# Linear attention beside a gather: the gates go from GpSimd to ScalarE, and GpSimd's adds move one iteration on

## The chip, the cores and the metric

The kernel runs on one core of a Trainium2 chip. The metric is the device time of one execution in microseconds. Before the change the median of three runs is 2528.86 us (2523.08 to 2537.23). The profiled execution took 2537.77 us, its span from the first to the last instruction is 2536.0 us, so 1.8 us lie around the span. All durations below come from that execution.

## The reference

Two transformer layers on X of shape 8 x 1024 x 128 (8192 tokens). What the change touches is the seam between them: the end of the first layer's mixture of experts, and the second layer's attention.

```
# layer 0, experts: every token has two experts with the gates w0, w1
out0 = all_out[n, top2_i[:, 0]]
out1 = all_out[n, top2_i[:, 1]]
moe_out = w[:, 0:1] * out0 + w[:, 1:2] * out1
result = clip(x + moe_out, -100, 100)        # x: the normalised token
# layer 1, linear attention, 16 heads of 8, causal sums over the tokens
q, k = relu(x Wq) + EPS, relu(x Wk) + EPS ;  v = x Wv
kv_cum = cumsum(k outer v) ;  k_cum = cumsum(k)
out = (q . kv_cum) / (q . k_cum + EPS) ; y = out @ Wo.T
```

Then a router picks one of eight experts for each token.

## The kernel before, in words

The program is a row of stages, each a block with one instruction stream per engine, kept in step by semaphores: projections, softmax attention, routing, experts of layer 0, `linear` (the stage of the change), capacity, experts of layer 1. The order of the instructions is written out by hand; no scheduler moves any.

`linear` works on 64 tiles of 128 tokens, four tiles to a group, so 16 groups. `groups` runs `iteration(g)` on every engine: four iterations (-2 to 1) written out, a loop of six rounds with two iterations each (groups 2 to 13), four more written out. In iteration g, for t = 0 to 3, the engines do the following.

- GpSimd: `keep_state(g, t)` (two small products, once ScalarE has copied the running sum, `raw`), then `outer` for the next tile (t+1, or tile 0 of the next group): the outer products k x v of a tile, 1024 columns. At t = 0 it copies the slot numbers of group g+2 (`take_slots`), and at t = 0, 1, 2 it issues 3, 3 and 2 indirect DMAs (`gather`) that fetch two expert rows for each of the 512 tokens of group g+2. At t = 3, `gate(g+2)`: multiply the rows by their gates (L1400), add the two rows of a token (L1404), add the normalised token (L1408), giving `moe`.
- VectorE: `features` of the next tile (L1685), `attend_tile(g, t)` (L1692 to L1718), and at t = 0 the block that begins with `clip(g+1)` (L1647), which waits for `moe` of group g+1, with `add_moe`, the statistics of the first norm and seven steps of the router between them. At t = 1 and 2 come the scales of both norms.
- ScalarE: `keep_sums` (`raw`, L1582), `keep_values` of the next tile (`v`, L1588 and L1589), `keep_queries` (`qT`, L1595), and at certain t roots, exponentials, whole-group copies and the normalised rows (`normalise`, L1610).
- TensorE: per tile the running state, the projection two tiles ahead, the turned q, the causal sums `p_cum` (`sums`, L1481) from the outer products and the share of the earlier tiles, `p_prev` (L1493).

The handovers that matter below: `outer` waits for `v`, `v` for `features`; `sums` waits for `outer`; `attend_tile` waits for `sums`; `keep_state` waits for `raw` and for `p_prev`; `clip` waits for `moe`. The rows and slots have two buffers, `moe` has one; the gate values lie in `GATE` for all tokens.

Of the kernel before, what the change touches and what calls it, by code (L numbers as in the profile page):

```python
# [22 lines left out]
ALU = mybir.AluOpType  # L23
# [3 lines left out]
P = 128  # L27
# [3 lines left out]
G = 4  # L31
# [36 lines left out]
def apart(eng, sem, value, passed):  # L68

    eng.wait_ge(sem, value)  # L70
    eng.sem_inc(passed, 1)  # L71
# [1197 lines left out]
def linear(nc, c, X, XN, GATE, SLOT, BESTP, HOT, W1, w, ys):  # L1269
# [5 lines left out]
    with ExitStack() as ctx:  # L1275
        def sb(name, shape, dt=F32):
            return ctx.enter_context(nc.sbuf_tensor(f"ln_{name}", shape, dt))
# [3 lines left out]
        def ps(name, shape):  # L1281
            return ctx.enter_context(nc.psum_tensor(f"ln_{name}", shape, F32))

        wqkv, wo, wr = sb("wqkv", [P, 3 * D]), sb("wo", [P, D]), sb("wr", [P, E1])
        slot = [sb(f"slot{i}", [P, G * 2], I32) for i in range(2)]
        rows = [sb(f"rows{i}", [P, G * 2, D]) for i in range(2)]
        moe = sb("moe", [P, G, D])

# [18 lines left out]
            "w_in", "ones", "mask", "x_a", "x_c", "stats_a", "stats_c", "var_a", "var_c", "root_a", "root_c",  # L1307
            "rstd_a", "rstd_c", "xn_a", "xn_c", "pxT_a", "pxT_c", "xT_a", "xT_c", "qkv", "qk", "v", "pqT", "qT",
            "kc", "kv", "st", "raw", "state", "cum", "prev", "prod", "o", "poT", "oT", "y", "kept", "logits", "shift",
            "exp", "passed", "w1_in", "moe", "clip", "den", "num", "slots", "gated", "top", "router")}  # L1310
        rows_in = [sem(f"rows_in{i}") for i in range(2)]
        passed = S["passed"]
        block = ctx.enter_context(nc.Block())
# [5 lines left out]
        def number(g):  # L1319
            return g[0] * 2 + g[1]  # L1320
# [43 lines left out]
        @block.gpsimd  # L1364
        def _(pool):
            def masked(out, keys, reps):

                nc.gpsimd.memset(out, 1.0).then_inc(S["mask"], 1)
                pool.wait_ge(S["mask"], keys + 1)
                nc.gpsimd.affine_select(out=out, in_=out, compare_op=ALU.is_ge, fill=0.0, base=0,  # L1370
                                        pattern=[[-DH1, H1], [0, reps]], channel_multiplier=1).then_inc(S["mask"], 1)
                pool.wait_ge(S["mask"], keys + 2)
                nc.gpsimd.affine_select(out=out, in_=out, compare_op=ALU.is_ge, fill=0.0, base=DH1 - 1,
                                        pattern=[[DH1, H1], [0, reps]], channel_multiplier=-1).then_inc(S["mask"], 1)

            masked(own_head[:, 0:D].rearrange("p (h m) -> p h m", h=H1), 0, DH1)
            masked(own_head[:, D:D + H1].rearrange("p (h m) -> p h m", h=H1), 3, 1)
            for i in range(2):
                nc.gpsimd.memset(v1[i][:, D:D + 1], 1.0).then_inc(S["ones"], 1)

            def take_slots(g):

                n, i = number(g), g[1]
                nc.gpsimd.tensor_copy(slot[i][:, :], SLOT[:, bass.ds(n * G * 2, G * 2)]).then_inc(S["slots"], 1)
                apart(pool, S["slots"], n + 1, passed)
                if not (isinstance(n, int) and n < 2):
                    apart(pool, S["moe"], n - 1, passed)

            def gather(g, t):
                i = g[1]  # L1390
                for n in ((0, 1, 2), (3, 4, 5), (6, 7), ())[t]:
                    pool.indirect_dma_start(rows[i][:, n, :], None, ys[:, :],  # L1392
                                            bass.IndirectOffsetOnAxis(ap=slot[i][:, n:n + 1], axis=0)).then_inc(rows_in[i], 16)

            def gate(g):
                b, i = g
                n = number(g)
                two = rows[i][:, :, :].rearrange("p (t k) d -> p t k d", k=2)
                apart(pool, rows_in[i], (b + 1) * G * 2 * 16, passed)
                nc.gpsimd.tensor_tensor(rows[i][:, :, :], rows[i][:, :, :],  # L1400
                                        GATE[:, bass.ds(number(g) * G * 2, G * 2)].unsqueeze(2).broadcast_to([P, G * 2, D]),
                                        ALU.mult).then_inc(S["gated"], 1)
                pool.wait_ge(S["gated"], 2 * n + 1)
                nc.gpsimd.tensor_tensor(two[:, :, 0, :], two[:, :, 0, :], two[:, :, 1, :], ALU.add).then_inc(S["gated"], 1)  # L1404
                if not (isinstance(n, int) and n == 0):
                    apart(pool, S["x_a"], n, passed)
                apart(pool, S["gated"], 2 * n + 2, passed)
                nc.gpsimd.tensor_tensor(moe[:, :, :], two[:, :, 0, :], group_of(XN, g), ALU.add).then_inc(S["moe"], 1)  # L1408

            def keep_state(g, t):  # L1410
                n = tile_number(g, t)
                apart(pool, S["raw"], n + 1, passed)
                if not (isinstance(n, int) and n == 0):
                    apart(pool, S["prev"], prevs(g[0], g[1] * G + t), passed)
                nc.gpsimd.tensor_tensor(state[:, 0:D], raw[:, 0:D], own_head[:, 0:D], ALU.mult).then_inc(S["state"], 1)
                nc.gpsimd.tensor_tensor(state[:, D:D + H1], own_head[:, D:D + H1], raw[:, D:D + 1].broadcast_to([P, H1]), ALU.mult).then_inc(S["state"], 1)

            def outer(g, t):
                n = tile_number(g, t)
                pool.wait_ge(S["v"], n + 1)  # L1420
                from_first(pool, "cum", n - 1)
                shape = [P, H1, DH1, DH1]
                k = qk[t % 2][:, D:2 * D].rearrange("p (h d) -> p h d", h=H1)
                v = v1[t % 2][:, 0:D].rearrange("p (h m) -> p h m", h=H1)
                nc.gpsimd.tensor_tensor(kv[t % 2][:, 0:KV1].rearrange("p (h m d) -> p h m d", h=H1, m=DH1),  # L1425
                                        k.unsqueeze(2).broadcast_to(shape), v.unsqueeze(3).broadcast_to(shape),
                                        ALU.mult).then_inc(S["kv"], 1)

            def iteration(g):
                for t in range(G):  # L1430
                    nxt = next_tile(g, t)
                    if exists(g):
                        keep_state(g, t)
                    if exists(nxt[0]):
                        outer(*nxt)
                    if exists(after(g, 2)):
                        if t == 0:
                            take_slots(after(g, 2))
                        gather(after(g, 2), t)
                        if t == 3:  # L1440
                            gate(after(g, 2))

            pool.wait_ge(S["mask"], 6)
            pool.sem_inc(passed, 1)
            groups(pool, iteration)
# [112 lines left out]
        def _(act):  # L1558
# [42 lines left out]
            def normalise(g, k):  # L1601
# [9 lines left out]
                                                bias=shift[k][:, t:t + 1], scale=rstd[k][:, t:t + 1])  # L1611
                last.then_inc(S[f"xn_{k}"], 1)

            def iteration(g):
                before = after(g, -1)
                for t in range(G):
# [20 lines left out]
                        normalise(after(g), "a")  # L1637
                    if t == 2 and exists(before):
                        normalise(before, "c")

            groups(act, iteration)

# [425 lines left out]
```

## Time and profile before

| | |
|---|---|
| median of 3 runs | 2528.86 us |
| the profiled execution | 2537.77 us |
| its span | 2536.0 us |
| TensorE busy | 1976.8 us (78%) |
| VectorE busy | 1680.6 us (66%) |
| ScalarE busy | 1055.1 us (42%) |
| GpSimd busy | 1688.4 us (67%) |
| granted TensorE clock, mean | 0.867 of full speed |

The shares are means over stages with different limits. The linear stage runs from about 1687 to about 2175 us of the span. A timeline row gives the start of an instruction in microseconds from the span's start, its duration, engine, line, operation and tiles, and in brackets how long the engine had been idle before it and what released it ("issue" where the profile shows nothing that it waited for). A start that follows another by less than that one's duration means that the two overlap in the pipeline.

### The profile page before, as it was taken

How to read it: one execution, taken by the hardware profiler on the slowest of the kernel's cores; microseconds unless marked ns; L12 is line 12 of the kernel's file. 1: busy time of each engine (PE TensorE's matmuls, PEld its weight loads, DVE VectorE, ACT ScalarE, POOL GpSimd, SP SyncE). 2: the span in 40 equal slices, each digit the busy share in tenths (PEclk: the TensorE clock that was granted, in tenths of full speed). 3: DMA queues.
4: the chain of work that ended last, by engine and by line, in shares of the span. 5: the costliest groups of instructions: out<-in, count | busy, mean ns of one | idle time of the engine just before them, and what ended most of it. 6: DMA issues, size and time to landing. Idle time of an engine off the chain costs nothing. (4 is left out here: it accounts for less than half of the span.)

```text
span 2536.0 us, 48665 instructions
## 1 busy us (share of the span) xinstructions
PE 1976.8 (78%) x12588; PEld 1077.1 (42%) x12588; DVE 1680.6 (66%) x4398; ACT 1055.1 (42%) x1662; POOL 1688.4 (67%) x1184
## 2 busy tenths in 40 slices
PE   7969999999999999999764529956667777320698
PEld 3423333333333333333254518843344444210597
DVE  7857777777777777777365653426888888550354
ACT  4534555555555555555432315522444444112243
POOL 3436888888888888888736553348887875117365
PEclk9878999999999999999865559978998889555799
DMA  6763222222222122222022223440000000112232
GB/s 196 252 211 107 66 65 60 59 65 66 66 65 64 59 62 66 66 66 64 22 85 74 98 73 118 128 153 24 18 20 20 19 17 9 38 54 98 77 103 69
DMA packets 159727, 192.97 MB, mean 76 GB/s; under 512 B 28793, under 2 KB 113792, under 8 KB 159648
## 3 DMA queue, kind: packets, MB, share of 16 engines
q1 hardware_dynamic: 144816, 161.83, 20.8%
q0 software_dynamic: 13824, 29.43, 3.6%
q10 hardware_dynamic: 1008, 0.92, 0.1%
q14 instruction: 60, 0.49, 0.1%
q8 instruction: 19, 0.31, 0.1%
HBM read 110.48 MB, written 82.10 MB: 76 GB/s over the span
## 5 line engine op out<-in xcount | busy, mean ns | idle before, releaser
L598 DVE TENSOR_REDUCE halfmax<-p_m 128x1 f32<-128x512 f32 x1024 | 664.2, 680 | 246.8 <-PE p_m L486 245.6
L467 POOL TENSOR_TENSOR sum_p<-sum_p,probs 128x1024 f32<-128x1024 f32 x320 | 754.7, 2358 | 39.9 <-ACT probs L593 19.7
L593 ACT ACTIVATE probs<-p_s 128x1024 f32<-128x1024 f32 x512 | 522.2, 1024 | 484.1 <-PE p_s L511 400.8
L486 PE MATMUL p_m<-ka,qa 128*128 128x512 bf16 x1024 | 397.0, 388 | 39.3 <-DVE halfmax L598 18.4
L510 PE MATMUL p_s<-qa,ka 128*128 128x512 bf16 x1024 | 391.4, 382 | 1.5 <-ACT probs L593 0.9
L511 PE MATMUL p_s<-qb,kb 66*128 66x512 bf16 x1024 | 390.9, 382 | 0.0
L518 PE MATMUL p_o<-probs,vh 128*32 128x256 f32 x4096 | 274.0, 385 | 0.0
L467 POOL TENSOR_TENSOR sum_p<-probs 128x1024 f32<-128x1024 f32 x64 | 150.3, 2348 | 138.1 <-ACT probs L593 138.1
L1481 PE MATMUL ln_p_cum<-ln_kv,c_tri 128*128 128x512 f32 (+1 forms) x384 | 167.4, 579 | 55.6 <-POOL ln_kv L1425 55.6
L1051 POOL DMA_INDIRECT xs<-r_xn,r_slot x128 | 124.6, 973 | 120.5 <-DVE r_slot L1015 85.4
L486 PEld LDWEIGHTS p_m<-ka,qa 128*128 128x128 bf16 x1024 | 99.6, 97 | 244.4 <-DVE halfmax L598 150.0
L1135 ACT ACTIVATE e_h<-e_p_h,e_w 128x256 f32<-128x256 f32 x316 | 126.4, 474 | 164.2 <-PE e_p_h L1114 90.3
L510 PEld LDWEIGHTS p_s<-qa,ka 128*128 128x128 bf16 x1024 | 100.1, 98 | 177.6 <-issue 99.8
L1114 PE MATMUL e_p_h<-e_xT,e_w 128*128 128x256 f32 x632 | 162.6, 392 | 5.0 <-DVE e_xT L1129 5.0
L1122 PE MATMUL e_p_y<-e_w,e_h 128*128 128x128 f32 x1264 | 163.2, 277 | 3.0 <-ACT e_h L1135 3.0
L518 PEld LDWEIGHTS p_o<-probs,vh 128*32 128x32 f32 x4096 | 106.8, 109 | 127.8 <-issue 44.4
L1392 POOL DMA_INDIRECT ln_rows<-ys,ln_slot x128 | 125.4, 979 | 46.4 <-issue 27.5
L1122 PEld LDWEIGHTS e_p_y<-e_w,e_h 128*128 128x128 f32 x1264 | 151.5, 193 | 7.6 <-issue 7.2
L1107 PE MATMUL e_p_xT<-c_ident,e_xb 128*128 128x128 f32 x236 | 46.7, 281 | 134.1 <-DMA e_xb<-xs 134.1
L1175 POOL DMA_INDIRECT out<-e_y,e_row_of x80 | 92.0, 1150 | 79.5 <-DVE e_y L1149 63.3
L1481 PEld LDWEIGHTS ln_p_cum<-ln_kv,c_tri 128*128 128x128 f32 x384 | 78.6, 219 | 155.9 <-issue 130.7
L511 PEld LDWEIGHTS p_s<-qb,kb 66*128 66x128 bf16 x1024 | 99.4, 97 | 93.4 <-issue 1.9
(277 smaller groups left out, 3110.3 us busy)
## 6 DMA issues: line engine op xcount, KB each, us to landing
qa<-q SPq DMA_DIRECT2D x128, 128.0 KB, 2.6
ka<-k SPq DMA_DIRECT2D x128, 128.0 KB, 2.8
e_xb<-xs SPq DMA_DIRECT2D x40, 257.0 KB
e_xb<-xs SPq DMA_DIRECT2D x78, 128.0 KB, 2.0
ys<-e_y SPq DMA_DIRECT2D x78, 128.0 KB, 1.9
v<-pj_v SPq DMA_DIRECT2D x8, 1024.0 KB, 5.0
qb<-q SPq DMA_DIRECT2D x64, 128.0 KB, 2.8
kb<-k SPq DMA_DIRECT2D x64, 128.0 KB, 2.9
```

What stands on the lines that cost most here:

```text
L467: nc.gpsimd.tensor_tensor(sum_p[s % 2][:, :], (sum_p[s % 2] if n else probs[0])[:, :], probs[k][:, :], ALU.add).then_inc(sum_p_d, 1)
L486: nc.tensor.matmul(max_bank(s, n)[:, :], qa[s][:, (n // 2) * P:(n // 2 + 1) * P], ka[s][:, (n % 2) * HALF:(n % 2 + 1) * HALF], start=True, ...
L510: nc.tensor.matmul(p_s[k % 2][:, q], ka[s][:, cols], qa[s][:, q], start=True, stop=False)
L511: mm = nc.tensor.matmul(p_s[k % 2][:, q], kb[s][:, cols], qb[s][:, q], start=False, stop=True)
L518: mm = nc.tensor.matmul(p_o[s % 2][j * DH0:(j + 1) * DH0, col, :], lhs, rhs[:, j * Q:(j + 1) * Q], start=start, stop=stop, skip_group_chec ...
L593: nc.scalar.activation(probs[k][:, :], p_s[k % 2][:, :], ACT.Exp, scale=SCALE).then_inc(probs_d, 1)
L598: nc.vector.reduce_max(halfmax[s % 2][:, n % 2, n // 2:n // 2 + 1], max_bank(s, n)[:, :], AX.X).then_inc(max_read, 1)
L1114: mm = nc.tensor.matmul(p_h[s % 2][:, f, :], w1[s][:, f * P:(f + 1) * P], xT[s % 2][:, :], start=True, stop=True)
L1122: mm = nc.tensor.matmul(p_y[s % 2][:, t * P:(t + 1) * P], h[s % 2][:, f, t * P:(t + 1) * P], w2[s][:, f, :], start=(f == 0), stop=(f == NF ...
L1135: last = nc.scalar.activation(h[s % 2][:, f, :], p_h[s % 2][:, f, :], act_fn, bias=b1[s][:, f:f + 1])
L1392: pool.indirect_dma_start(rows[i][:, n, :], None, ys[:, :], bass.IndirectOffsetOnAxis(ap=slot[i][:, n:n + 1], axis=0)).then_inc(rows_in[i] ...
L1481: mm = nc.tensor.matmul(p_cum[:, a, 0:z], c["tri"][:, :], kv[t % 2][:, a * 512:a * 512 + z], start=True, stop=True)
```

## The change

ScalarE gets a new function `weigh(g)`: eight activations (Identity) that multiply the eight row blocks of a group, 128 x 128 each, by the gate as a scale per partition. It is called at the end of t = 3, for group g+2 in iteration g, and waits for the gathered rows. GpSimd loses the multiply (L1400), keeps the two adds (now `gate(g+1)`) and does them at t = 0 of the next iteration, behind `keep_state` and `outer` of that t and ahead of `take_slots`. [...] `gated` now counts groups weighed by ScalarE, and `pair` is a new semaphore for GpSimd's first add.

```diff
--- before.py
+++ after.py
@@ -1283,6 +1283,7 @@
 
         wqkv, wo, wr = sb("wqkv", [P, 3 * D]), sb("wo", [P, D]), sb("wr", [P, E1])
         slot = [sb(f"slot{i}", [P, G * 2], I32) for i in range(2)]
+        share = [sb(f"share{i}", [P, G * 2]) for i in range(2)]
         rows = [sb(f"rows{i}", [P, G * 2, D]) for i in range(2)]
         moe = sb("moe", [P, G, D])
 
@@ -1307,7 +1308,7 @@
             "w_in", "ones", "mask", "x_a", "x_c", "stats_a", "stats_c", "var_a", "var_c", "root_a", "root_c",
             "rstd_a", "rstd_c", "xn_a", "xn_c", "pxT_a", "pxT_c", "xT_a", "xT_c", "qkv", "qk", "v", "pqT", "qT",
             "kc", "kv", "st", "raw", "state", "cum", "prev", "prod", "o", "poT", "oT", "y", "kept", "logits", "shift",
-            "exp", "passed", "w1_in", "moe", "clip", "den", "num", "slots", "gated", "top", "router")}
+            "exp", "passed", "w1_in", "moe", "clip", "den", "num", "slots", "gated", "pair", "top", "router")}
         rows_in = [sem(f"rows_in{i}") for i in range(2)]
         passed = S["passed"]
         block = ctx.enter_context(nc.Block())
@@ -1381,6 +1382,8 @@
             def take_slots(g):
 
                 n, i = number(g), g[1]
+                from_first(pool, "gated", n - 1)
+                nc.gpsimd.tensor_copy(share[i][:, :], GATE[:, bass.ds(n * G * 2, G * 2)])
                 nc.gpsimd.tensor_copy(slot[i][:, :], SLOT[:, bass.ds(n * G * 2, G * 2)]).then_inc(S["slots"], 1)
                 apart(pool, S["slots"], n + 1, passed)
                 if not (isinstance(n, int) and n < 2):
@@ -1396,15 +1399,11 @@
                 b, i = g
                 n = number(g)
                 two = rows[i][:, :, :].rearrange("p (t k) d -> p t k d", k=2)
-                apart(pool, rows_in[i], (b + 1) * G * 2 * 16, passed)
-                nc.gpsimd.tensor_tensor(rows[i][:, :, :], rows[i][:, :, :],
-                                        GATE[:, bass.ds(number(g) * G * 2, G * 2)].unsqueeze(2).broadcast_to([P, G * 2, D]),
-                                        ALU.mult).then_inc(S["gated"], 1)
-                pool.wait_ge(S["gated"], 2 * n + 1)
-                nc.gpsimd.tensor_tensor(two[:, :, 0, :], two[:, :, 0, :], two[:, :, 1, :], ALU.add).then_inc(S["gated"], 1)
+                apart(pool, S["gated"], n + 1, passed)
+                nc.gpsimd.tensor_tensor(two[:, :, 0, :], two[:, :, 0, :], two[:, :, 1, :], ALU.add).then_inc(S["pair"], 1)
                 if not (isinstance(n, int) and n == 0):
                     apart(pool, S["x_a"], n, passed)
-                apart(pool, S["gated"], 2 * n + 2, passed)
+                apart(pool, S["pair"], n + 1, passed)
                 nc.gpsimd.tensor_tensor(moe[:, :, :], two[:, :, 0, :], group_of(XN, g), ALU.add).then_inc(S["moe"], 1)
 
             def keep_state(g, t):
@@ -1433,12 +1432,12 @@
                         keep_state(g, t)
                     if exists(nxt[0]):
                         outer(*nxt)
+                    if t == 0 and exists(after(g)):
+                        gate(after(g))
                     if exists(after(g, 2)):
                         if t == 0:
                             take_slots(after(g, 2))
                         gather(after(g, 2), t)
-                        if t == 3:
-                            gate(after(g, 2))
 
             pool.wait_ge(S["mask"], 6)
             pool.sem_inc(passed, 1)
@@ -1610,6 +1609,15 @@
                     last = nc.scalar.activation(xn[k][:, t, :], group_of(X, g)[:, t, :], ACT.Identity,
                                                 bias=shift[k][:, t:t + 1], scale=rstd[k][:, t:t + 1])
                 last.then_inc(S[f"xn_{k}"], 1)
+
+            def weigh(g):
+                b, i = g
+                n = number(g)
+                apart(act, rows_in[i], (b + 1) * G * 2 * 16, passed)
+                act.wait_ge(S["slots"], n + 1)
+                for m in range(G * 2):
+                    last = nc.scalar.activation(rows[i][:, m, :], rows[i][:, m, :], ACT.Identity, scale=share[i][:, m:m + 1])
+                last.then_inc(S["gated"], 1)
 
             def iteration(g):
                 before = after(g, -1)
@@ -1637,6 +1645,8 @@
                         normalise(after(g), "a")
                     if t == 2 and exists(before):
                         normalise(before, "c")
+                    if t == 3 and exists(after(g, 2)):
+                        weigh(after(g, 2))
 
             groups(act, iteration)
```

GpSimd in the loop of before, from the last gathers of an iteration (t = 2) to the gating at its end (`ln_kv` is the outer product, `ln_state` is keep_state, `ln_rows` the gathered rows):

```order
L1392 DMA ln_rows0<-ys0,ln_slot0 128x128 x2
L70 REGISTER_ALU
L1415 TENSOR_TENSOR ln_state<-ln_raw,ln_own_head 128x128
L1416 TENSOR_TENSOR ln_state<-ln_own_head,ln_raw 128x16
L1420 ISA
L1328 REGISTER_ALU
L1425 TENSOR_TENSOR ln_kv0<-ln_qk0,ln_v1_0 128x1024
L70 ISA
L1400 REGISTER_ALU
L1400 TENSOR_TENSOR ln_rows0<-ln_rows0,GATE 128x1024
L1403 ISA
L1404 TENSOR_TENSOR ln_rows0<-ln_rows0 128x4x128
```

The same engine after the change, from the outer product of tile 0 (t = 3) to the two copies that precede the next gathers:

```order
L1424 TENSOR_TENSOR ln_kv0<-ln_qk0,ln_v1_0 128x1024
L70 REGISTER_ALU
L1414 TENSOR_TENSOR ln_state<-ln_raw,ln_own_head 128x128
L1415 TENSOR_TENSOR ln_state<-ln_own_head,ln_raw 128x16
L1419 REGISTER_ALU
L1424 TENSOR_TENSOR ln_kv1<-ln_qk1,ln_v1_1 128x1024
L1403 TENSOR_TENSOR ln_rows0<-ln_rows0 128x4x128
L1407 ISA
L1407 TENSOR_TENSOR ln_moe<-ln_rows0,XN 128x512
L1386 ISA
L1386 COPY ln_share1<-GATE 128x8
L1387 REGISTER_ALU
```

Before, the gating stood between the outer product of tile 0 and the keep_state of t = 0; now that keep_state follows the outer product at once, and the two adds stand behind the outer product of tile 1.

ScalarE in the loop after the change, at the seam of two iterations:

```order
L1594 COPY ln_qT0<-ln_p_T 128x128
L70 ISA
L1617 ISA
L1619 ACTIVATE ln_rows0<-ln_rows0,ln_share0 128x128 x8
L1329 REGISTER_ALU
L1581 COPY ln_raw<-ln_p_st 128x129
L1585 REGISTER_ALU
L1587 COPY ln_v1_1<-ln_p_qkv 128x128
```

The eight activations stand between the `qT` copy of t = 3 and the `raw` and `v` copies of t = 0; before, the `raw` copy came right behind `qT`. VectorE's and TensorE's orders are as before.

## Rows read from the trace of the kernel before

**Rows 1.** 110 us of the linear stage: busy us (x instructions) by engine, clock, DMA share, GB/s.
```profile
1830.00:1940.00 110.00, 77.41 (x304) 45.42 (x303) 91.80 (x333) 46.52 (x128) 87.44 (x94) 0.91 0.08 20
```

**Rows 2.** Timeline, GpSimd, a group without the loop's branch: start us, us, what [idle before].
```profile
1912.42 1.95 POOL L1425 TENSOR_TENSOR ln_kv<-ln_qk,ln_v 128x1024 f32<-128x1024 f32 x1
1914.33 1.94 POOL L1400 TENSOR_TENSOR ln_rows<-ln_rows,GATE 128x1024 f32<-128x1024 f32 x1
1916.35 1.27 POOL L1404 TENSOR_TENSOR ln_rows<-ln_rows 128x512 f32<-128x512 f32 x1
1917.89 1.27 POOL L1408 TENSOR_TENSOR ln_moe<-ln_rows,XN 128x512 f32<-128x512 f32 x1 [0.26 <-POOL ln_rows L1404]
1919.11 0.45 POOL L1415 TENSOR_TENSOR ln_state<-ln_raw,ln_own_head 128x128 f32<-128x128 f32 x1
...
1919.70 1.94 POOL L1425 TENSOR_TENSOR ln_kv<-ln_qk,ln_v 128x1024 f32<-128x1024 f32 x1
1921.60 0.25 POOL L1384 COPY ln_slot<-SLOT 128x8 int32 x1
...
1927.09 1.94 POOL L1425 TENSOR_TENSOR ln_kv<-ln_qk,ln_v 128x1024 f32<-128x1024 f32 x1
...
1940.41 1.95 POOL L1425 TENSOR_TENSOR ln_kv<-ln_qk,ln_v 128x1024 f32<-128x1024 f32 x1
```

**Rows 3.** Timeline, VectorE, the same group.
```profile
1920.21 1.58 DVE L1718 TENSOR_TENSOR ln_o<-ln_num,ln_den 128x128 f32<-128x128 f32 x1 [0.18 <-DVE ln_den L1714]
1921.72 0.41 DVE L1647 TENSOR_SCALAR ln_moe<-ln_moe 128x512 f32<-128x512 f32 x1
...
1925.94 0.42 DVE L1685 TENSOR_SCALAR ln_qk<-ln_p_qkv 128x256 f32<-128x256 f32 x1
...
1929.60 0.29 DVE L1718 TENSOR_TENSOR ln_o<-ln_num,ln_den 128x128 f32<-128x128 f32 x1
...
1933.41 0.29 DVE L1692 TENSOR_TENSOR ln_prod<-ln_p_cum,ln_qk 128x128 f32<-128x128 f32 x1 [0.63 <-PE ln_p_cum L1481]
```

**Rows 4.** Timeline, ScalarE, the same group.
```profile
1914.12 0.27 ACT L1595 COPY ln_qT<-ln_p_T 128x128 f32<-128x128 f32 x1 [0.86 <-PE ln_p_T L1472]
1914.28 0.27 ACT L1582 COPY ln_raw<-ln_p_st 128x129 f32<-128x129 f32 x1
```

**Rows 5.** Timeline, TensorE, the same group.
```profile
1929.17 4.20 PE L1481 MATMUL ln_p_cum<-ln_kv,c_tri 128*128 128x512 f32 x6 [0.74 <-POOL ln_kv L1425]
```

**Rows 6.** Timeline, VectorE, the group behind the loop's branch.
```profile
1889.54 0.42 DVE L1685 TENSOR_SCALAR ln_qk<-ln_p_qkv 128x256 f32<-128x256 f32 x1 [2.89 <-issue]
...
1894.02 0.42 DVE L1647 TENSOR_SCALAR ln_moe<-ln_moe 128x512 f32<-128x512 f32 x1
...
1898.66 0.41 DVE L1685 TENSOR_SCALAR ln_qk<-ln_p_qkv 128x256 f32<-128x256 f32 x1
```

**Rows 7.** Timeline, GpSimd, the group behind the loop's branch.
```profile
1891.50 1.96 POOL L1425 TENSOR_TENSOR ln_kv<-ln_qk,ln_v 128x1024 f32<-128x1024 f32 x1
...
1899.45 1.95 POOL L1425 TENSOR_TENSOR ln_kv<-ln_qk,ln_v 128x1024 f32<-128x1024 f32 x1 [0.73 <-ACT ln_v L1588]
```

**Rows 8.** Groups by line and form, ScalarE, 1830 to 2050 us: busy us, mean ns.
```profile
L1610 ACT ACTIVATE ln_xn_a<-X,ln_shift_a,ln_rstd_a 128x128 f32 x32 | 13.2, 482 | 19.2 <-DVE ln_shift_a L1678 19.2
...
L1589 ACT COPY ln_kv<-ln_qk 128x128 f32<-128x128 f32 x31 | 9.3, 301 | 0.0
...
L1570 ACT COPY XN<-ln_xn_c 128x512 f32 x7 | 4.4, 622 | 0.0
```

**Rows 9.** Timeline, ScalarE, in the first expert stage.
```profile
1608.09 0.84 ACT L1135 ACTIVATE e_h<-e_p_h,e_w 128x256 f32<-128x256 f32 x2 [1.45 <-PE e_p_h L1114]
```

**Rows 10.** Timeline, GpSimd, start of the linear stage.
```profile
1703.23 1.90 POOL L1400 TENSOR_TENSOR ln_rows<-ln_rows,GATE 128x1024 f32<-128x1024 f32 x1 [4.50 <-DMA ln_rows<-ys,ln_slot]
```

**Rows 11.** Timeline, GpSimd, from the last gating to the next group.
```profile
2110.74 1.96 POOL L1425 TENSOR_TENSOR ln_kv<-ln_qk,ln_v 128x1024 f32<-128x1024 f32 x1
...
2137.48 1.95 POOL L1425 TENSOR_TENSOR ln_kv<-ln_qk,ln_v 128x1024 f32<-128x1024 f32 x1
```

## The prediction

> **What bounds the kernel now.** I read the busy time by stretch first, then the timelines of the four engines over the 15 us around the gating, then the rows of forms for prices. In the linear stage GpSimd is busy 87.4 of 110 us and VectorE 91.8 [rows 1], so both are near their limit there and neither share settles which one sets the pace. The timelines do.
>
> I call O0, O1 and O2 the outer products of tiles 0, 1 and 2 of a group. In a group without the loop's branch O0 starts at 1912.42, O1 at 1919.70, O2 at 1927.09 and the next O0 at 1940.41 [rows 2], 27.99 us for the group. From O0 to O1 GpSimd works without a gap: 1.95 for O0, 4.8 for the gating, 0.6 for keep_state. From O1 to O2 it issues the slot copy, three gathers and keep_state, and O2 starts at 1927.09. VectorE runs beside it: clip at 1921.72 opens the block that ends in `features` of tile 2 at 1925.94 (4.22 us later) [rows 3], whose values ScalarE can hand on at about 1926.7. So GpSimd's queue sets O2, but only 0.4 us later than VectorE's would. In the group behind the loop's branch VectorE first stands idle for 2.89 us, ahead of `features` at 1889.54 [rows 6], and O2 waits for ScalarE's `v`, which hangs on VectorE's block (0.73 us idle) [rows 7]. There VectorE sets the pace. A third witness: in the last group with a gating in it no gathers are issued any more (about 10 us less work on GpSimd), yet it still takes 2137.48 - 2110.74 = 26.74 us from O0 to O0 [rows 11]. Taking work from GpSimd can therefore give at most about 1.25 us per group; two chains of nearly equal length run through this stage, and a delay of either shows.
>
> **What the change removes.** 16 multiplies of 1.94 us on GpSimd [rows 2]. It adds one small copy per group, 0.2 us, priced like the slot copy (0.25) [rows 2]. That is 1.75 us less work per group.
>
> **What it adds on ScalarE.** Eight activations in a row. The price of one is bounded by the normalising row, the same operation and size with two operands per partition: 0.482 us alone and 13.2 / 32 = 0.41 us apiece in rows of four, where neighbours overlap [rows 8], so about 0.40 apiece in a row of eight. From below by the plain copy of 128 columns, which starts 0.16 us ahead of its follower [rows 4]. The nearest is the experts' activation with one operand per partition and 256 columns, two in 0.84 us [rows 9], 0.42 each; 128 columns fewer take off 0.107 us, since 384 columns make 0.622 - 0.301 = 0.321 us [rows 8]. I take 0.30 apiece, 2.4 us for the eight (1.3 and 3.2 are the ends). The Trainium skill, page ScalarE: Activation LUTs, section What ACT_TABLE_LOAD costs, gives 186 ns + 0.833 ns per column, 93 ns more per pointer operand and 93 ns of overlap, by which the eight would be an estimated 2.4 us; the row with two pointers agrees (it would be 479 ns), no row here has one pointer and 128 columns.
>
> **Where it stands.** Before the change `raw` of tile 0 follows `qT` at once: 1914.12 and 1914.28 [rows 4], and nobody needs it until 1919.11, since GpSimd is gating [rows 2]. So the gating covered the wait for `raw`. After it, GpSimd finishes O0 at 1914.37 and needs `raw` immediately. The rows have landed by then (the gating of before started on them at 1914.33 without waiting). Step by step, group without branch:
> - the eight activations from 1914.4 to 1916.8; `raw` to 17.0; handover 0.35, an estimate whose nearest row is the 0.26 us of the second add behind the first [rows 2]
> - keep_state at 1917.35, O1 at 1917.95 (it was 1919.70, so 1.75 us earlier), to 1919.9
> - the adds: 1.54 and 1.27 us [rows 2], `moe` at 1922.7
> - clip at 1922.8. It was at 1921.72 [rows 3]: 1.1 us late. Before, `moe` was ready at 1919.1; now the last step of clip's wait is the adds, behind O1
> - the block of 4.22 us follows, so `features` of tile 2 is 1.1 us late
> - on GpSimd the `share` copy, then 1921.60 to 1927.09 again (5.49 us) [rows 2]: O2 at 1922.7 + 0.2 + 5.5 = 1928.4, 1.25 us late
> - the sums of tile 2 took 4.20 us at the lower clock and VectorE waited 0.63 us for them [rows 3, 5]. If that remains, the second half is 1.25 late; if they run at the higher clock (2.2 us), VectorE's own 1.1 less the 0.63 is what is left, about 0.4.
> I take 1.1 us per such group. Queued behind the wait of clip on VectorE are the statistics, the router's steps and `features`, and ScalarE, TensorE and GpSimd all wait for the last of them.
>
> Group behind the branch: with O0 7.3 us ahead of O1, as in the other group, `raw` ends at 1884.2 + 2.0 + 2.4 + 0.3 = 1888.9, inside VectorE's idle 2.89 us, so the activations are hidden. `v` of tile 1 still waits for `features` at 1889.54 [rows 6] and lands at 1890.3, O1 starts then (1891.50 before [rows 7]) and ends at 1892.3, the adds end at 1895.1, while clip was at 1894.02 and `features` followed 4.64 us later [rows 6]. Clip is 1.1 late, and 0.3 more because VectorE's last product of tile 0 has two SBUF inputs and meets the adds. That is 1.4 us, and it doesn't depend on the activations' price. O2 hung on VectorE there already, so it passes on whole.
>
> That such a product waits for GpSimd can be read: `ln_o` of tile 0 took 1.58 us and ended at 1921.79, just behind O1 at 1921.64, while `ln_o` of tile 1, beside no work of GpSimd but DMA issues, took 0.29 us [rows 2, 3].
>
> **The sum.** Start of the stage: gather, wait, multiply 1.90 us [rows 10] becomes 2.4 us of activations, 0.1 of handover and 0.2 of the copy, 0.8 us late. Iterations 0 to 14 have the adds in them. Of the five branches back each is followed by one, 5 x 1.4 = 7.0; the ten others 10 x 1.1 = 11.0. Together 18.8 us. The profiled execution of 2537.8 us would become 2556.6; it stood 8.9 us above the median, so the median goes from 2528.9 to 2547.7. Nothing outside the stage changes.
>
> Bounds: below, copies' price of 0.16 us an activation (clip then at 1921.8, no delay without branch, 0.2 from the GpSimd copy) gives -0.3 + 5 x 1.2 + 10 x 0.2 = 8 us or, with the sums of tile 2 at the higher clock, 6. Above: 0.40 us an activation makes O2 0.8 to 0.9 later than in the steps, 2.2 us, and with the sums of tile 2 at the lower clock in every group the ones behind a branch lose 2.0, so 1.6 + 5 x 2.0 + 10 x 2.2 = 34 us. Below nothing goes only what the first two rivals give.
>
> **Rivals.**
> 1. *GpSimd is the bound and gets its 1.75 us.* For: no gap from O0 to O2 without branch. Against: 0.4 us of slack only, and the 26.74 us group [rows 11]. It would be limited to 1.25 x 15 = 19 us: 2510.
> 2. *VectorE is freed of GpSimd's port.* The Trainium skill, page SBUF — State Buffer, section SBUF: two separate sides, says that GpSimd and a VectorE operation with two SBUF inputs exclude each other for a whole instruction; by that rule alone the time would fall, and the trace agrees with the exclusion. In this kernel's terms: O1 ends 1.75 us earlier, `ln_o` of tile 0 would no longer wait 1.3 us in ten groups, 13 us: 2516. It pays only if `moe` is ready by 1920.5, for which the activations would have to take nearly nothing. Together with rival 1: 0.10.
> 3. *Hidden after all.* Activations near 0.16 us, the sums of tile 2 at the higher clock, 6 to 8 us more: 2536. For: VectorE has 0.63 us of idle time to give back per group. 0.18.
> 4. *ScalarE as the serial step.* The eight take 3.2 us, `raw`, `v` and the turned output of each group come late, the lower clock follows TensorE's longer pauses: 34 us, 2563. From 2.9 us of activations on it decides. 0.12.
>
> **How the numbers follow.** The forecast has 0.60. Half a per cent is 12.6 us and about what a measurement can tell from no change. Slower by more: most of the forecast (0.52) and rival 4, 0.64. Within: the rest of the forecast and most of rival 3 and a little of the first two, 0.26. Faster: 0.10. The range runs from 2530 (no gain, hardly a loss) to 2565 (rival 4): it leaves out the two fast rivals and a tail above.
>
> **What would show it.** Right: clip (`ln_moe` on VectorE) waits 1 to 2 us for GpSimd's second add in nearly every group, where before only the first waited; GpSimd waits about 3 us for `raw` behind O0 without branch; the eight activations take 2.4 us; O0 to O0 is 29.1 us without and 29.6 with a branch. Wrong: clip doesn't wait, groups of 27 us or less, or activations that wait for gathered rows, which would make it slower than forecast.

## The result and the profile after

The change makes the kernel slower: 2544.82 us against 2529.16 us (medians of 8 runs each), ratio 1.0063, 95% interval 1.0050 to 1.0077. Forecast was 2547.7 against 2528.9. The profiled execution took 2553.63 us. Its page, the span and the busy time by engine:

```profile
span 2551.9 us, 48803 instructions
...
PE 1975.8 (77%) x12588; PEld 1074.1 (42%) x12588; DVE 1681.2 (66%) x4398; ACT 1090.1 (43%) x1790; POOL 1657.9 (65%) x1184
```

GpSimd is busy 30.5 us less than before, ScalarE 35.0 us more, and the span is 15.9 us longer. The same stretch of the linear stage as in [rows 1], moved by ten microseconds:

```profile
1840.00:1950.00 110.00, 75.42 (x298) 43.92 (x297) 91.80 (x332) 52.97 (x153) 79.83 (x92) 0.91 0.07 20
```

GpSimd fell from 87.4 to 79.8 of 110 us while VectorE stayed at 91.8. What was taken from GpSimd has turned into waiting, as the timelines show.

The seam of two iterations in a group without the loop's branch, which answers to [rows 2]. GpSimd's timeline (start, duration, engine, line, operation and tiles, and in brackets the idle time before it and its releaser; `ln_share` is the copy of the group's gates that the diff adds to `take_slots`):

```profile
1923.47 0.46 POOL L1414 TENSOR_TENSOR ln_state<-ln_raw,ln_own_head 128x128 f32<-128x128 f32 x1 [2.96 <-ACT ln_raw L1581]
...
1924.06 1.95 POOL L1424 TENSOR_TENSOR ln_kv<-ln_qk,ln_v 128x1024 f32<-128x1024 f32 x1
1925.97 1.27 POOL L1403 TENSOR_TENSOR ln_rows<-ln_rows 128x512 f32<-128x512 f32 x1
1927.50 1.26 POOL L1407 TENSOR_TENSOR ln_moe<-ln_rows,XN 128x512 f32<-128x512 f32 x1 [0.27 <-POOL ln_rows L1403]
1928.71 0.19 POOL L1386 COPY ln_share<-GATE 128x8 f32 x1
1928.84 0.43 POOL L1387 COPY ln_slot<-SLOT 128x8 int32 x1
...
1934.28 1.95 POOL L1424 TENSOR_TENSOR ln_kv<-ln_qk,ln_v 128x1024 f32<-128x1024 f32 x1
```

O0 of this group starts at 1918.55. Keep_state (`ln_state`) waits 2.96 us for `raw`, O1 starts at O0 + 5.51 (before: + 7.28), the adds follow, and `moe` is there at 1928.76, that is O0 + 10.2 (before: O0 + 6.7, since 1917.89 + 1.27 = 1919.16). VectorE's timeline of that group, answering to [rows 3]:

```profile
1926.35 1.04 DVE L1728 TENSOR_TENSOR ln_o<-ln_num,ln_den 128x128 f32<-128x128 f32 x1 [0.18 <-DVE ln_den L1724]
1928.80 0.43 DVE L1657 TENSOR_SCALAR ln_moe<-ln_moe 128x512 f32<-128x512 f32 x1 [1.42 <-POOL ln_moe L1407]
...
1933.04 0.42 DVE L1695 TENSOR_SCALAR ln_qk<-ln_p_qkv 128x256 f32<-128x256 f32 x1
...
1940.26 0.29 DVE L1702 TENSOR_TENSOR ln_prod<-ln_p_cum,ln_qk 128x128 f32<-128x128 f32 x1 [0.39 <-issue]
```

Clip (`ln_moe`) now waits 1.42 us for the second add and starts at O0 + 10.25 instead of O0 + 9.30; `features` follows 4.24 us later, as before (4.22). `ln_o` took 1.58 us beside O1 before; O1 now lies ahead of it, but the first add stands beside it, and it still takes 1.04 us. O2 starts at 1934.28, O0 + 15.7 instead of + 14.7. The last row is the wait for the sums of tile 2 [rows 3], 0.39 us where it was 0.63: they ran for the most part at the lower level again (granted clock 0.50 from 1933 to 1939), but `ln_prod` comes only 0.72 us later than before, counted from O0. ScalarE, answering to [rows 4]:

```profile
1920.26 0.27 ACT L1594 COPY ln_qT<-ln_p_T 128x128 f32<-128x128 f32 x1 [0.87 <-PE ln_p_T L1471]
1920.54 2.44 ACT L1619 ACTIVATE ln_rows<-ln_rows,ln_share 128x128 f32<-128x128 f32 x8
1922.89 0.24 ACT L1581 COPY ln_raw<-ln_p_st 128x129 f32<-128x129 f32 x1
```

The eight activations start behind `qT`, take 2.44 us in all and put `raw` 2.47 us later behind `qT`.

**Where the 15.9 us lie.** With O0 of the first and the last group as marks (1716.41 and 2151.93 us, before 1718.91 and 2137.48): groups 0 to 14 take 435.52 instead of 418.57 us, +16.95. Of these the five groups behind a branch (4, 6, 8, 10, 12) took 149.86 instead of 144.48, +5.4, and the ten others 285.66 instead of 274.09, +11.6. The start, from the stage's first small copy (1684.61; before 1687.81) to the first O0, takes 31.80 instead of 31.10, +0.7. Everything behind the last O0 adds 1.45, and the stages ahead of the linear one were 3.2 us shorter in this execution, which the change doesn't touch: 16.95 + 0.7 + 1.45 - 3.2 = 15.9. What the 1.45 us come from was not looked into. In the ten groups without a branch O2 comes 0.92 to 1.07 us later behind O0 in every one, 10.1 us of their 11.6; the rest of a group, from O2 to the next O0, takes between 11.5 and 13.3 us, with no pattern that I found.

### The profile page after: what moved, and what is told of

Its sections match the earlier page's. It is cut to its first block and busy times, and to the rows that moved or that the text cites. A ratio compares the mean times of both kernels' runs of the same rounds, so it can differ in the third digit from the quotient of the medians.

```text
span 2551.9 us, 48803 instructions
## 1 busy us (share of the span) xinstructions
PE 1975.8 (77%) x12588; PEld 1074.1 (42%) x12588; DVE 1681.2 (66%) x4398; ACT 1090.1 (43%) x1790; POOL 1657.9 (65%) x1184
## 5 line engine op out<-in xcount | busy, mean ns | idle before, releaser
L467 POOL TENSOR_TENSOR sum_p<-probs 128x1024 f32<-128x1024 f32 x64 | 150.2, 2347 | 138.8 <-ACT probs L593 138.8
L486 PEld LDWEIGHTS p_m<-ka,qa 128*128 128x128 bf16 x1024 | 99.5, 97 | 245.1 <-DVE halfmax L598 150.2
L1395 POOL DMA_INDIRECT ln_rows<-ys,ln_slot x128 | 123.1, 961 | 46.2 <-issue 28.6
L620 DVE RECIPROCAL inv<-p_o 128x128 f32<-128x128 f32 x128 | 120.9, 946 | 24.5 <-PE p_o L518 24.5
```

Source lines behind the costliest of these rows:

```text
L467: nc.gpsimd.tensor_tensor(sum_p[s % 2][:, :], (sum_p[s % 2] if n else probs[0])[:, :], probs[k][:, :], ALU.add).then_inc(sum_p_d, 1)
L486: nc.tensor.matmul(max_bank(s, n)[:, :], qa[s][:, (n // 2) * P:(n // 2 + 1) * P], ka[s][:, (n % 2) * HALF:(n % 2 + 1) * HALF], start=True, ...
L1395: pool.indirect_dma_start(rows[i][:, n, :], None, ys[:, :], bass.IndirectOffsetOnAxis(ap=slot[i][:, n:n + 1], axis=0)).then_inc(rows_in[i] ...
```

## The experiments

All ratios are to the kernel before on the same chip, where it took 2475.6 to 2478.9 us. A table of what the traces show, for group 7 (no branch) and group 6 (behind a branch); "sum" is the time from O0 of group 0 to O0 of group 15, worked out from the starts of `ln_kv`. No trace of the kernel before was taken on the later chips; e2, whose ratio is near 1, stands in for it.

| kernel | ratio [95%] | O0 to O1, g7 | O0 to clip, g7 | group 7 | group 6 | sum |
|---|---|---|---|---|---|---|
| before (first chip) | 1 | 7.28 | 9.30 | 27.99 | 28.23 | 418.6 |
| change (first chip) | 1.0063 | 5.51 | 10.25 | 28.69 | 29.52 | 435.5 |
| e8 change | 1.0081 [1.0068, 1.0095] | 5.50 | 10.23 | 28.18 | 29.72 | 433.1 |
| e1 no multiply | 0.9914 [0.9897, 0.9931] | 5.31 | 8.00 | 26.09 | 27.72 | 400.5 |
| e2 idle activations | 0.9989 [0.9978, 0.9999] | 7.28 | 9.30 | 27.63 | 28.22 | 415.6 |
| e3 adds first | 1.0039 [1.0026, 1.0052] | 7.94 | 8.05 | 28.72 | 29.33 | 428.8 |
| e4 one activation | 1.0027 [1.0017, 1.0038] | 5.30 | 10.04 | 28.00 | 29.99 | 425.8 |
| e5 split, old place | 0.9948 [0.9934, 0.9961] | 5.31 | 8.00 | 26.22 | 27.79 | 399.4 |
| e6 split, new place | 1.0053 [1.0039, 1.0067] | 5.30 | 10.05 | 28.06 | 29.96 | 426.6 |
| e7 gating moved | 1.0154 [1.0140, 1.0167] | 5.30 | 12.01 | 30.22 | 31.30 | 453.6 |
| e9 two states | 0.9984 [0.9975, 0.9993] | 3.46 | 8.25 | 27.03 | 29.51 | 415.0 |
| e10 change, two states | 1.0060 [1.0046, 1.0074] | 5.50 | 10.24 | 28.54 | 29.57 | 432.6 |
| e11 e5 with two states | 0.9919 [0.9905, 0.9932] | 5.29 | 7.99 | 26.60 | 27.92 | 398.7 |

**e1: the multiply alone left out.**

```diff
-                nc.gpsimd.tensor_tensor(rows[i][:, :, :], rows[i][:, :, :],
-                                        GATE[...].broadcast_to([P, G * 2, D]), ALU.mult).then_inc(S["gated"], 1)
-                pool.wait_ge(S["gated"], 2 * n + 1)
```

> The kernel before with GpSimd's multiply left out and nothing put in its place (so the rows are added without their gates); the two adds stay at t = 3. It measures what 1.94 us per group less on GpSimd are worth at most. Theory (two chains of nearly equal length): O0 to O1 falls from 7.3 to 5.4 us, the product ln_o of tile 0 no longer waits for O1 (0.3 instead of 1.6 us), clip comes about 1.2 us earlier, then VectorE's chain sets the rest: 0.8 to 1.5 us per group, 12 to 20 us, about 2513. Rival, GpSimd alone sets the pace: 15 x 1.94 = 29 us, 2500. Rival, VectorE alone sets the pace: no change, 2529.

Measured 0.9914, 21 us of 2479 (17 to 26 by the interval), a little over the range of the theory (12 to 20) and below the 29 of the rival in which GpSimd alone sets the pace; that of VectorE alone is out. VectorE at the end of tile 0, group 7:

```profile
1858.39 0.29 DVE L1714 TENSOR_TENSOR ln_o<-ln_num,ln_den 128x128 f32<-128x128 f32 x1 [0.18 <-DVE ln_den L1710]
1858.60 0.42 DVE L1643 TENSOR_SCALAR ln_moe<-ln_moe 128x512 f32<-128x512 f32 x1
```

`ln_o` takes 0.29 us where it took 1.58 [rows 3], since O1 now lies ahead of it, and clip starts at O0 + 8.00. Between the marks the trace is 15.1 us shorter than that of e2 (18.1 against the kernel before on the first chip), so the 1.94 us were worth 1.0 to 1.2 us per group, provided that the adds stay where they are. The start of the stage gives 2 us more (29.21 us from the first small copy to the first O0, 31.43 in e2); the rest of the 21 isn't located.

**e2: eight activations on ScalarE at the changed kernel's place, the gating as before.**

```diff
+        spare = sb("spare", [P, G * 2, D])
...
+            def idle(g):
+                for m in range(G * 2):
+                    nc.scalar.activation(spare[:, m, :], c["tri"][:, :], ACT.Identity, scale=c["ones"][:, m:m + 1])
...
+                    if t == 3 and exists(after(g, 2)):
+                        idle(after(g, 2))
```

> The kernel before with eight activations of 128 x 128 at the end of ScalarE's t = 3 that read a constant and write a tile that nobody reads; the gating stays on GpSimd at its old place. It asks whether 2.44 us on ScalarE cost anything while the gating still stands between O0 and keep_state. Theory (the gating of 4.8 us covers the wait for raw): 0 to 3 us, 2530, GpSimd does not wait for raw behind the gating. Rival, the activations lie on the path by themselves, through v and the turned output: 10 to 17 us, 2543.

Measured 0.9989, so no cost. GpSimd behind the gating, group 7:

```profile
1866.66 1.27 POOL L1409 TENSOR_TENSOR ln_moe<-ln_rows,XN 128x512 f32<-128x512 f32 x1 [0.26 <-POOL ln_rows L1405]
1867.89 0.46 POOL L1416 TENSOR_TENSOR ln_state<-ln_raw,ln_own_head 128x128 f32<-128x128 f32 x1
```

Keep_state follows the last add without idle time: 4.8 us of gating cover `raw` even when it comes 2.4 us later.

**e3: the adds ahead of keep_state and O1.**

```diff
+                    if t == 0 and exists(after(g)):
+                        gate(after(g))
                     if exists(g):
                         keep_state(g, t)
                     if exists(nxt[0]):
                         outer(*nxt)
-                    if t == 0 and exists(after(g)):
-                        gate(after(g))
```

> The changed kernel with the two adds ahead of keep_state and O1 at t = 0 instead of behind O1; ScalarE is unchanged. Clip then no longer waits, since moe is ready at O0 + 7.6 us, but O1 moves from O0 + 5.5 to O0 + 8.2. Theory (GpSimd's queue behind the late activations costs as much as clip's wait): O2 comes at O0 + 15.7, the same as in the changed kernel, 12 to 17 us above before, 2543. Rival, the price is clip's wait on VectorE alone: 2530, as before.

Measured 1.0039: of the two the theory, but it overstated the loss (0.5 to 0.7% expected), and the kernel is faster than the change (e8). The adds now wait for the eight activations, and O1 behind them starts at O0 + 7.94. Clip doesn't wait for `moe` any more, yet it gains little, as VectorE's row and GpSimd's O1 beside it show:

```profile
1874.74 2.16 DVE L1657 TENSOR_SCALAR ln_moe<-ln_moe 128x512 f32<-128x512 f32 x1
```

```profile
1874.63 2.00 POOL L1424 TENSOR_TENSOR ln_kv<-ln_qk,ln_v 128x1024 f32<-128x1024 f32 x1
```

Clip takes 2.16 us instead of 0.42 and ends at 1876.90, just behind O1 at 1876.63. It reads and writes SBUF only. The rows show that it ends with GpSimd's product; that it stands still meanwhile is how I read them.

**e4: one activation of eight.** The edit is `for m in range(1)` in `weigh`; seven of eight row blocks stay ungated.

> The changed kernel with one of the eight activations (seven of eight row blocks keep their ungated values); waits, orders and the adds behind O1 are those of the changed kernel. Theory (the eight activations ahead of raw make everything behind them late; the place of the adds alone costs nothing): raw 2.0 us earlier, O0 to O1 about 3.8 us without a branch, clip at O0 + 8.5, O2 at O0 + 14.2: 6 to 14 us below before, about 2519. Rival, adds behind O1 are too late for clip whatever ScalarE does: clip still waits over 1 us, 2540.

Measured 1.0027, at odds with the theory and nearer to the rival. GpSimd's keep_state of tile 0 and the TensorE row that releases it, group 7:

```profile
1867.39 0.46 POOL L1414 TENSOR_TENSOR ln_state<-ln_raw,ln_own_head 128x128 f32<-128x128 f32 x1 [2.76 <-PE ln_p_prev L1492]
```

```profile
1866.80 0.41 PE L1492 MATMUL ln_p_prev<-ln_state,ln_qT 128*128 128x144 f32 x2
```

`raw` is early now, but keep_state overwrites the small state tile, and TensorE reads the old one in `p_prev` only behind the sums of tile 0, at O0 + 4.5. That wait was hidden under the gating before, just as `raw` was, and I had not seen it. In the odd groups from 3 on the seven activations therefore cost 0.2 us (5.50 against 5.30), and clip waits 1.42 us for the adds with or without them. In the even groups without a branch (0, 2, 14) there is no `p_prev` for tile 0 of a batch, and there the seven activations are worth 2 us each (group 2: 29.09 in e8, 27.11 here).

**e9: e4 with two buffers for the state tile.**

```diff
-                    apart(pool, S["prev"], prevs(g[0], g[1] * G + t), passed)
+                    apart(pool, S["prev"], seen, passed)      # seen = prevs(g[0], g[1] * G + t - 1)
-                nc.gpsimd.tensor_tensor(state[:, 0:D], ...)
+                nc.gpsimd.tensor_tensor(state[t % 2][:, 0:D], ...)
...
-                nc.tensor.matmul(p_prev[:, 0:D + H1], qT[t % 2][:, :], state[:, :], ...)
+                nc.tensor.matmul(p_prev[:, 0:D + H1], qT[t % 2][:, :], state[(t + 1) % 2][:, :], ...)
```

> The run with one activation of eight, with two buffers for the small state tile, so that keep_state of tile 0 no longer waits until TensorE has read the state of the tile before (p_prev). In the run with one activation keep_state sat idle 2.76 us for that in groups without a branch, and O0 to O1 was 5.3 us although raw was early. Theory (p_prev holds keep_state there): O0 to O1 falls to 3.5 to 4.0 us in the odd groups, clip comes 1.3 us earlier in each, the even groups keep 6.1 us since they wait for v: 8 x 1.3 = 10 us less than with one state, ratio 0.997 to 1.000 against 1.0027. Rival (something else holds O1): 1.0027 again.

The row blocks stay ungated as in e4. Measured 0.9984, 0.43% less than e4, and O0 to O1 is 3.46 us. Keep_state and O1, group 7, with O0 at 1856.47:

```profile
1859.34 0.46 POOL L1415 TENSOR_TENSOR ln_state<-ln_raw,ln_own_head 128x128 f32<-128x128 f32 x1 [0.92 <-ACT ln_raw L1582]
...
1859.93 1.95 POOL L1425 TENSOR_TENSOR ln_kv<-ln_qk,ln_v 128x1024 f32<-128x1024 f32 x1
```

It waits for `raw` again, 0.92 us. The wait for `p_prev` is thereby shown. The five groups behind a branch hardly moved together (150.2 us, 150.5 in e4): O1 waits for `v` there.

**e10: the changed kernel with two buffers for the state tile.** The edit is that of e9.

> The changed kernel with all eight activations and two buffers for the state tile. Theory (raw behind the eight activations and p_prev come within 0.2 us of each other, so that removing one wait leaves the other): O0 to O1 stays at 5.5 us in the odd groups, ratio 1.007 to 1.009 as the changed kernel (1.0081). Rival (p_prev alone holds it): 1.002 to 1.005.

Measured 1.0060, below the expected 1.007 to 1.009 and above the rival's range; the interval overlaps that of e8 (1.0081), so a small gain elsewhere is possible and not settled. At the seam nothing moved, the wait is that of the changed kernel to the digit:

```profile
1872.79 0.46 POOL L1415 TENSOR_TENSOR ln_state<-ln_raw,ln_own_head 128x128 f32<-128x128 f32 x1 [2.96 <-ACT ln_raw L1582]
```

So `raw` (behind eight activations) and `p_prev` are two waits of nearly one length, side by side. Removing one leaves the other; with both removed (e9) the seam shortens by 2 us.

**e7: the whole gating on GpSimd, moved behind O1.** The edit moves the call of `gate` from t = 3 to t = 0 of the next iteration, for group g+1, as in the change.

> The kernel before with the whole gating (multiply and both adds, all on GpSimd) moved behind O1 of t = 0 of the next iteration; ScalarE does nothing for it. Theory (what stands behind O1 delays clip one for one): moe at about O0 + 5.3 + 1.9 + 4.8 = 12.1, clip 2.7 us later than before in every group and O2 with it, 15 x 2.7 = 40 us, ratio 1.014 to 1.018. Rival (the place costs nothing, only the activations do): 0.998 to 1.002.

Measured 1.0154, inside the expected range. VectorE, group 7:

```profile
1887.51 0.43 DVE L1647 TENSOR_SCALAR ln_moe<-ln_moe 128x512 f32<-128x512 f32 x1 [2.75 <-POOL ln_moe L1408]
```

Clip waits 2.75 us and comes at O0 + 12.01. ScalarE does nothing for the gating here: the place alone costs 1.5%. The change then takes 1.9 us of GpSimd's work out of that chain again (O0 to clip 10.23) and ends at +0.8%.

**e8: the change unaltered.**

> The changed kernel unaltered, for a ratio on the chip of these experiments. Expected 1.005 to 1.008 of before, as in the first comparison. Theory (the two adds behind O1 are the price, about 0.2 us per group comes from the activations): 0.2 to 0.4% above the run with one activation, whose ratio was 1.0027. Rival (the activations are the price): over 0.6% above it.

Measured 1.0081, 0.54% above e4 with its seven activations fewer. By the sums of the traces it is 7.3 us in the groups (three even groups of 2 us, the rest in the odd ones) and 2 us at the start of the stage, 0.4% together. The theory's 0.2 to 0.4% was low; the difference lies between the two accounts.

**e5: the activations split, the adds back at t = 3.**

```diff
-rows_in = [sem(f"rows_in{i}") for i in range(2)]
+rows_in = [[sem(f"rows_in{i}_{p}") for p in range(3)] for i in range(2)]
...
+                    if t == 3 and exists(after(g, 2)):
+                        weigh(after(g, 2), 2)                 # row blocks 6, 7
                     if exists(next_tile(g, t)[0]):
                         keep_queries(*next_tile(g, t))
+                    if t in (1, 2) and exists(after(g, 2)):
+                        weigh(after(g, 2), t - 1)             # blocks 0 to 2 and 3 to 5
...
                         gather(after(g, 2), t)
+                        if t == 3:
+                            gate(after(g, 2))
```

> The change with two edits: the eight activations are split by the gather that feeds them (three at the end of ScalarE's t = 1 ahead of the normalisation, three at t = 2 likewise, two at t = 3 ahead of the qT copy), each with its own semaphore, and the two adds go back to t = 3 behind O0. ScalarE waits 1.4 to 2.4 us at those places anyway, and the adds (2.8 us) end at O0 + 4.8, when keep_state can start in any case. Theory: nearly the gain of the run without the multiply (0.9914), less the share copy: ratio 0.992 to 0.995, clip without a wait at O0 + 8, O0 to O1 5.3 us without a branch. Rival, the pieces delay raw, v and the normalised rows or wait for gathered rows: 0.998 to 1.004.

Measured 0.9948, faster than both kernels. ScalarE over one group (6), the three pieces among their neighbours:

```profile
1840.65 0.98 ACT L1620 ACTIVATE ln_rows<-ln_rows,ln_share 128x128 f32<-128x128 f32 x3
1843.31 1.65 ACT L1609 ACTIVATE ln_xn_a<-X,ln_shift_a,ln_rstd_a 128x128 f32 x4 [1.67 <-DVE ln_shift_a L1692]
...
1848.32 0.98 ACT L1620 ACTIVATE ln_rows<-ln_rows,ln_share 128x128 f32<-128x128 f32 x3
1849.22 1.63 ACT L1609 ACTIVATE ln_xn_c<-X,ln_shift_c,ln_rstd_c 128x128 f32 x4
...
1852.95 0.69 ACT L1620 ACTIVATE ln_rows<-ln_rows,ln_share 128x128 f32<-128x128 f32 x2
1853.91 0.27 ACT L1594 COPY ln_qT<-ln_p_T 128x128 f32<-128x128 f32 x1 [0.27 <-PE ln_p_T L1471]
```

The first piece lies in the wait for the norm's shift (`ln_xn_a` still waits 1.67 us behind it), the third in the wait for the turned q (0.27 us left), and the second takes the place of the wait that `ln_xn_c` had. GpSimd at the seam, group 7:

```profile
1855.68 1.28 POOL L1407 TENSOR_TENSOR ln_moe<-ln_rows,XN 128x512 f32<-128x512 f32 x1 [0.26 <-POOL ln_rows L1403]
1856.96 0.46 POOL L1414 TENSOR_TENSOR ln_state<-ln_raw,ln_own_head 128x128 f32<-128x128 f32 x1
```

The adds end and keep_state starts, as with the multiply left out (e1). The sum between the marks is that of e1 too (399.4 and 400.5 us); what e5 lacks against it lies partly ahead of them: from the stage's first small copy to the first O0 it takes 32.48 us, e1 29.21. ScalarE shows why: there the first piece of the second group stands ahead of the normalised rows and waits 3.18 us for its gathered rows, as the rival said, but only at the start:

```profile
1660.57 0.99 ACT L1620 ACTIVATE ln_rows<-ln_rows,ln_share 128x128 f32<-128x128 f32 x3 [3.18 <-DMA ln_rows<-ys,ln_slot]
1661.46 1.63 ACT L1609 ACTIVATE ln_xn_a<-X,ln_shift_a,ln_rstd_a 128x128 f32<-128x128 f32 x4
```

**e6: the split activations with the adds behind O1.**

> The split activations of the run before, but the two adds at the changed kernel's place behind O1. Theory (the place of the adds is the price): 1.002 to 1.004, like the run with one activation, clip waits over 1 us in groups without a branch. Rival (ScalarE's activations ahead of raw are the price): 0.992 to 0.996, like the split with the adds at the old place.

Measured 1.0053, above the theory's 1.002 to 1.004, and nowhere near the rival. e5 and e6 differ in one call only. VectorE, group 7:

```profile
1875.65 0.43 DVE L1661 TENSOR_SCALAR ln_moe<-ln_moe 128x512 f32<-128x512 f32 x1 [1.42 <-POOL ln_moe L1407]
```

The 1.42 us wait of clip is that of the changed kernel, though the eight activations no longer stand between `qT` and `raw`. The same chip gives 1.0053 here and 1.0081 for the change (e8), and the intervals don't overlap: of the 1.33% between e5 and the change 1.05 come with the adds' place and 0.28 with the place of the activations.

**e11: e5 with two buffers for the state tile.**

> The split activations with the adds at the old place (ratio 0.9948) and two buffers for the state tile besides. In the group's first tile the adds end when p_prev does, so nothing changes there; in the other tiles keep_state waits up to 1.4 us for p_prev, where VectorE's chain is mostly the longer one. Theory: 0 to 0.3% less, 0.992 to 0.995. Rival (p_prev holds the later tiles): under 0.990.

Measured 0.9919, at the theory's lower edge, and the best version: 20 us under the kernel before and 1.6% under the changed one. The seam is that of e5 (5.29 us); between the marks the traces differ by only 0.7 us, and the start of the stage takes 32.22 us instead of 32.48. Two buffers gain 0.29% in the ratio, 7 us, of which the marks and the start show 1. The two ratios come from two chips, so how much of the rest is a gain stays open.

## Why the prediction was right, and where not

The size and the sign were right: +15.7 us measured, +18.8 forecast. The step that carries the forecast, clip late behind the adds, was right; one cause in it was not (4), and how near the sums came is in part luck (2).

1. *Clip waits for the adds behind O1, about 1.1 us late, and O2 with it 1.25.* Right: it waits 1.3 to 1.4 us in every group without a branch from group 1 on (1.42 in group 7) and comes 0.95 us later in group 7; O2 comes 1.06 later (the working's own numbers give 1.31 and not 1.25: 1928.40 - 1927.09). e5 against e6, one call apart, shows that this place is the larger price.
2. *Ten groups 1.1 us, five groups 1.4 us, start 0.8.* Measured 1.16, 1.08 and 0.7 on average; single groups lie between 0.5 and 2.2 and between 0.0 and 2.2. The forecast of 29.1 us for a group without a branch took group 7 (27.99) for all ten, whose mean was 27.4; after the change it is 28.6. In the groups behind a branch clip shows no idle time; the delay sits in `ln_o` ahead of it, which ends with the second add. The first row is of the kernel before, the others of the changed one, both group 6:

```profile
1892.59 0.89 DVE L1712 TENSOR_SCALAR ln_den<-ln_den 128x16 f32<-128x16 f32 x1
...
1894.37 0.42 DVE L1695 TENSOR_SCALAR ln_qk<-ln_p_qkv 128x256 f32<-128x256 f32 x1 [2.90 <-issue]
...
1897.42 0.95 DVE L1722 TENSOR_SCALAR ln_den<-ln_den 128x16 f32<-128x16 f32 x1
...
1898.70 1.33 DVE L1728 TENSOR_TENSOR ln_o<-ln_num,ln_den 128x128 f32<-128x128 f32 x1
1899.95 0.41 DVE L1657 TENSOR_SCALAR ln_moe<-ln_moe 128x512 f32<-128x512 f32 x1
```

   `ln_den` was long before already (0.89 us for 16 columns, beside O1; 0.95 now, beside the first add). `ln_o` takes 1.33 us and took 0.29, and clip starts at O0 + 10.92 where it was + 9.83, 1.09 later and not 1.4: the 0.3 us that the working put on top for `ln_o` don't show. Of the five, group 4 lost nothing (29.55 before, 29.54 after), since it had been slow before (28.54 in e2), and group 12 lost 2.2.
3. *The activations take 2.4 us.* 2.44; the bounds of 1.3 and 3.2 were not needed.
4. *GpSimd needs `raw` at once, and the gating covered that wait.* Half right. e2 shows the cover. But the working treated `raw` as the only wait under it. `p_prev` holds keep_state until O0 + 4.7 (e4, group 7), 0.2 us less than the eight activations do, and so in all odd groups from 3 on. The term came out right while its cause did not, and that is luck: by the same reasoning I expected a gain of 6 to 14 us (0.2 to 0.6%) for one activation of eight, and e4 is at +0.27%. That is the step that was wrong, and it was in the open: the handovers listed ahead of the prediction say that keep_state waits for `p_prev`.
5. *Taking work from GpSimd can give at most 1.25 us per group* (the slow side of rival 1). The size was about right: between the marks e1 and e5 gain 15 and 16 us against e2's trace, 1.0 to 1.1 us per group (1.2 and 1.3 against the first chip's trace), and e1 21 us in all where the bound was 19. The reason was wrong. The group of 26.74 us [rows 11] was no bound, because it still had the whole gating at its start, and VectorE's `ln_o` still stood beside O1; in the same trace group 0 took 25.74 us, and without the multiply (e1) the groups without a branch take 24.1 to 26.5. Rival 2 had the other part of it, that VectorE is freed when O1 moves ahead of `ln_o`; in the changed kernel only half a microsecond of it came (`ln_o` 1.04 us instead of 1.58), and that was lost in the wait for `moe`, as it said.

## What to carry to other kernels

Before work is moved off a busy engine, list every wait that ends under that work, not only the nearest: the order of arrival decides what the engine does next, and two waits of nearly one length hide each other. What is left of the work should stay in the shadow of a wait that is there anyway (here the 2.8 us from the end of O0 to `p_prev`, as long as the two adds) unless its reader is late; the same edit was +0.8% with the adds behind the next product and -0.5% with them in the shadow and the moved part cut into pieces that lie in the new engine's own pauses. A busy share says nothing on this: 7.6 us less on GpSimd in 110 went with a slower kernel.

## What the runs showed of the hardware

- A VectorE operation that only touches SBUF can last as long as the GpSimd instruction beside it: clip 2.16 instead of 0.42 us in e3, `ln_den` on 16 columns 0.95 us in the changed kernel where it takes 0.16 in e5, each ending within 0.3 us of GpSimd's instruction. Not every one does: beside O1 of group 7 in the changed kernel the two reductions kept 0.28 and 1.21 us and the reciprocal 0.24. In e3 clip started 2.2 us earlier than in e8 and took 1.7 us longer, which ate most of what the removed wait had given.
- An activation of 128 x 128 with one operand per partition takes 386 ns (median of 128) and eight in a row 2.44 us.
- The same two kernels took 50 us less on the later chips (2544.8 and 2495.2 us for the change). The first O0 came at 1716.4 on the one and at 1668.5 us on the other, while the sum over the groups differs by 2.4 us, so most of it lies ahead of the linear stage: of the 61.0 us between the two profiled spans 47.9 lie ahead of the first O0 and 10.6 behind the last. What makes the chips differ is open. Only ratios taken on one chip are compared here.
- In group 12 the second indirect DMA is issued 1.8 to 2.2 us behind the end of the first instead of 0.30, in all thirteen traces, the kernel before among them (2.19). It costs more in the changed kernel: O1 to O2 takes 12.16 us there instead of the 10.4 of the other groups behind a branch, before 9.06 instead of the 7.95 of groups 6, 8 and 10. What causes it was not tried.
